# A Mamba block with a mixture of experts: softplus, router and buffers rearranged, and GpSimd's product by C as one operation for each state step

## What is computed

```python
xp, res = split(x @ W_in.T)                      # 512 and 512 channels
xc = silu(causal_conv4(xp) + conv_b)
B, C, dt = split(xc @ W_x.T)                     # 16, 16 and 1 per token
dt = softplus(dt @ W_dt.T + b_dt)                # 512 channels
h  = exp(-exp(A_log) * dt) * h + dt * B * xc     # scan over tokens; 512 channels x 16 states
y  = einsum(h, C) + D * xc                       # sum over the 16 states
x  = layernorm(x + silu(y + res) @ W_out.T)
p  = softmax(x @ router.T); w, idx = top_k(p, 2); w = w / (w.sum() + 1e-9)
x  = layernorm(x + sum_k w_k * expert_idx_k(x))  # w1: 256 -> 1024, gelu, w2: 1024 -> 256
```

## Time and profile before

| | |
|---|---|
| median of 3 runs | 1729.33 us (1729.17 to 1731.65) |
| the profiled execution: its own time | 1732.87 us |
| its span, first to last instruction | 1731.3 us |
| mean granted TensorE clock | 0.882 of full speed |
| busy: PE, DVE, ACT, POOL | 1373.5, 1191.1, 1046.8, 958.5 us |
| first scan starts, last scan ends | 82.3 and 1087.1 us |
| first product of the experts | 1167.8 us |

### The profile page before, as it was taken

The page is one execution under the profiler, slowest core; times in us unless marked ns, Lnnn a source line. Parts: engine busy times, 40 slices in busy tenths (PEclk is TensorE's granted clock), DMA queues, the critical chain, the costliest instruction groups (busy, mean ns, idle before and its releaser), DMA issues. The chain is left out here.

```text
span 1731.3 us, 29370 instructions
## 1 busy us (share of the span) xinstructions
PE 1373.5 (79%) x8770; PEld 1144.4 (66%) x8771; DVE 1191.1 (69%) x2152; ACT 1046.8 (60%) x1474; POOL 958.5 (55%) x823
## 2 busy tenths in 40 slices
PE   4487796796896797797888789618999999999950
PEld 1256575575675676675666677517888889898850
DVE  2377777777878778778768689335666666666648
ACT  1788888788868778868688777203333333333414
POOL 0088877787976877875777888441222222222228
PEclk8688898998988898888888889758999999999975
DMA  2032232232332232332232333166644441411125
GB/s 69 25 105 91 93 117 89 76 117 89 111 107 83 94 123 68 114 116 77 101 110 70 109 122 107 49 211 189 195 151 149 154 147 40 149 41 38 38 92 218
DMA packets 104873, 183.63 MB, mean 106 GB/s; under 512 B 13200, under 2 KB 40464, under 8 KB 104784
## 3 DMA queue, kind: packets, MB, share of 16 engines
q1 hardware_dynamic: 89968, 150.48, 26.7%
q0 software_dynamic: 9888, 27.29, 4.7%
q10 hardware_dynamic: 4928, 4.73, 0.8%
HBM read 121.23 MB, written 61.23 MB: 105 GB/s over the span
## 5 line engine op out<-in xcount | busy, mean ns | idle before, releaser
L1023 POOL TENSOR_TENSOR arena<-arena 128x1024 f32<-128x1024 f32 x256 | 610.4, 2389 | 105.7 <-DVE arena L798 94.9
L401 PE MATMUL d_ps<-ident,arena 128*128 128x128 f32 x2048 | 348.3, 298 | 84.7 <-DVE arena L798 74.8
L628 ACT ACTIVATE arena<-u_tok,b_tok 128x512 f32<-128x512 f32 x512 | 327.4, 712 | 140.0 <-PE d_ps L401 139.9
L401 PEld LDWEIGHTS d_ps<-ident,arena 128*128 128x128 f32 x2048 | 262.2, 153 | 222.4 <-issue 100.9
L798 DVE TENSOR_TENSOR_SCAN arena<-arena,d_ps 128x512 f32<-128x512 f32 x256 | 303.8, 1211 | 117.1 <-PE d_ps L401 115.4
L798 DVE TENSOR_TENSOR_SCAN arena<-arena,carry,d_ps 128x512 f32<-128x512 f32 x256 | 319.7, 1271 | 93.4 <-PE d_ps L401 91.0
L415 PE MATMUL y_ps<-ident,arena 128*128 128x128 f32 x2048 | 323.6, 288 | 12.7 <-POOL arena L1023 12.7
L1240 POOL DMA_INDIRECT expert_out<-y,dest x71 | 70.9, 999 | 378.3 <-PE xt_ps L1299 331.0
L638 ACT ACTIVATE arena<-dt,neg_a 128x2048 f32<-128x2048 f32 x128 | 255.3, 1995 | 24.7 <-DVE arena L798 24.5
L415 PEld LDWEIGHTS y_ps<-ident,arena 128*128 128x128 f32 x2048 | 258.8, 150 | 15.3 <-POOL arena L1023 15.2
L1273 ACT ACTIVATE h_t<-ht_ps 128x512 f32<-128x512 f32 x142 | 84.4, 595 | 303.7 <-PE ht_ps L1331 303.7
(11 more groups left out here) (165 smaller groups left out, 1639.6 us busy)
## 6 DMA issues: line engine op xcount, KB each, us to landing
arena<-c_rows SPq DMA_DIRECT2D x128, 256.0 KB, 3.1
weight_parts<-arena SPq DMA_DIRECT2D x128, 256.0 KB, 2.0
arena<-weight_parts SPq DMA_DIRECT2D x32, 1024.0 KB, 5.4
arena<-in_pieces SPq DMA_DIRECT2D x128, 128.0 KB, 2.4
xg<-expert_rows POOLq DMA_DIRECT2D x71, 130.0 KB, 2.4
c_y<-expert_out SPq DMA_DIRECT2D x16, 512.0 KB, 8.0
x_t<-in_x_t SPq DMA_DIRECT2D x8, 512.0 KB, 4.2
x_t<-in_x_tok SPq DMA_DIRECT2D x8, 512.0 KB, 4.6
```

Of the source, the lines that this page charges most:

```text
L401: last = nc.tensor.matmul(d_ps[:, c % 2, j * P:(j + 1) * P], ub[:, g % U_RING, j, c * P:(c + 1) * P], t.ident[:], start=True, stop=True, i ...
L628: nc.scalar.activation(ub[:, g % U_RING, j, :], u_tok[:, j, :], ACT.Identity, scale=b_tok[:, b % 2, j, n:n + 1]).then_inc(scaled, 1)
L1023: nc.gpsimd.tensor_tensor(h[:, g % H_RING, lo:hi, :], h[:, g % H_RING, lo:hi, :], c_row[:, g % C_RING:g % C_RING + 1, :].broadcast_to([P, ...
```

## The change

1. `times_c` is one operation of 2048 columns for each step, with one `carry` copy. It waits for the fourth scan, and `hc_done` counts once for each step; all four groups of `sum_states` wait for it. `SUM_AT` becomes 6 + k + max(0, 10 - k // 3) (the same from k = 30 on), and the ring of `h` has 5 tiles, not 4.
2. Softplus works in `pre`, not in `tmp`, and runs earlier: `z_parts` at n = 5 and 6, `soft_tail` at n = 7. `silu` and `y_silu` move to n = 2, ahead of `scale(g + 2)` in ACT's program; `y_silu` writes a tile of its own, `y_u`. The additions that make dt and dt times xc are four operations of 1024 columns, one behind each scan of n = 10. The taps lie one behind each scan at (11, 2) to (12, 3) and (0, 0) to (1, 1). `ut_out` is spread over n = 13 and 14.
3. The router picks from the logits themselves. DVE does max, index and one-hot (8 operations of 8 columns) at (3, 0); subtraction, denominator, weights and the product of the one-hot with the ranks go to POOL. All 8 indirect transfers of a block stand at n = 12 to 15. The last two operations of `variance` go to POOL. The halo's sums are made ahead, at n = 4 of the iteration before.
4. Buffers: `x_t` has 2 tiles, not 3. The raw weight pieces are loaded into the second half of `parts`, so a piece's load follows the store of the one two before it, one step ahead. `BANK_OF` has other banks, and block 0 uses four banks of `y_ps`, which is idle then.
5. `setup` no longer waits for its 12 loads: three groups with a semaphore each are waited for where they are used, and two of the loads are issued by ACT.

Core of the diff (the rest renames semaphores or moves lines as said):

```diff
-H_RING = 4
+H_RING = 5
...
-        SUM_AT = [6 + k + max(0, 6 - k // 3) for k in range(4 * STATE)]
+        SUM_AT = [6 + k + max(0, 10 - k // 3) for k in range(4 * STATE)]
...
                 def sum_states(b, k):
-                    pe.wait_ge(hc_done, 2 * g + half + 1)
+                    pe.wait_ge(hc_done, g + 1)
...
-            def times_c(g, half):
-                pool.wait_ge(scan_done, 4 * g + 2 * half + 2)
-                lo, hi = 2 * half, 2 * half + 2
+            def times_c(g):
+                pool.wait_ge(scan_done, 4 * g + 4)
                 if b % 2 == 0:
-                    nc.gpsimd.tensor_copy(carry[:, n, lo:hi].unsqueeze(2), h[:, g % H_RING, lo:hi, T - 1:T])\
+                    nc.gpsimd.tensor_copy(carry[:, n, :].unsqueeze(2), h[:, g % H_RING, :, T - 1:T])\
...
-                nc.gpsimd.tensor_tensor(h[:, g % H_RING, lo:hi, :], h[:, g % H_RING, lo:hi, :],
-                                        c_row[:, g % C_RING:g % C_RING + 1, :].broadcast_to([P, 2, T]), ALU.mult)\
+                nc.gpsimd.tensor_tensor(h[:, g % H_RING], h[:, g % H_RING],
+                                        c_row[:, g % C_RING:g % C_RING + 1, :].broadcast_to([P, EC, T]), ALU.mult)\
                     .then_inc(hc_done, 1)
...
-                def step_sizes():
-                    dve.wait_ge(ln_done, 2 * f + 2)
-                    nc.vector.tensor_tensor(dt[:, f % 2], dt[:, f % 2], tmp[:], ALU.add).then_inc(dt_done, 1)
-                    nc.vector.tensor_tensor(tmp[:], dt[:, f % 2], xc[:, f % 2], ALU.mult).then_inc(u_done, 1)
+                def add_sizes(half):
...
+                    nc.vector.tensor_tensor(dt[:, f % 2, lo:hi], dt[:, f % 2, lo:hi], pre[:, lo:hi], ALU.add)\
+                        .then_inc(dt_done, 1)
+                def inputs(half):
...
+                    last = nc.vector.tensor_tensor(y_u[:, lo:hi], dt[:, f % 2, lo:hi], xc[:, f % 2, lo:hi], ALU.mult)
...
+                def router_pick():
+                    for j in range(TT):
+                        last = nc.vector.max(top[:, j, :], logit[:, j, :])
+                    for j in range(TT):
+                        last = nc.vector.max_index(idx[:, j, :], top[:, j, :], logit[:, j, :])
+                    for j in range(TT):
+                        for k in range(TOPK):
+                            last = nc.vector.tensor_scalar(onehot[:, j, k, :], t.iota_ef[:], ek[:, j, k:k + 1], None,
+                                                           ALU.is_equal)
...
                 for n in range(STATE):
                     g = STATE * i + n
+                    if back and n == 2:
+                        y_silu()
+                    if front:
+                        if n == 2:
+                            silu()
+                        if n == 7:
+                            soft_tail()
                     if 0 <= g + LEAD < STEPS:
                         scale(g + LEAD)
                         decays(g + LEAD)
                     if scans:
                         high_part(g)
...
                     if 0 <= g - 1 < STEPS:
-                        times_c(g - 1, 1)
+                        times_c(g - 1)
                     if scans:
-                        times_c(g, 0)
                         low_part(g)
...
-                    if place and n >= 14:
-                        send_rows(i - 2, n - 14)
+                        if n >= 12:
+                            send_rows(p, n - 12)
```

More of the change, by code:

```diff
@@ L129, with bank_of @@
             **{u: 2 for u in ("in0", "in1", "in2", "in3")}}
+EARLY_BANK = {**{f"in{c}": 2 + c for c in range(4)}, **{f"ut{j}": 2 + j for j in range(4)}}
+BANKS = 6
+def bank_of(use, b):
+    return EARLY_BANK[use] if b == 0 and use in EARLY_BANK else BANK_OF[use]
 def bank_counts():
-    fills, count = [0, 0], {}
+    fills, count = [0] * BANKS, {}
     for i in range(-2, BLOCKS + 2):
-        for u, bank in BANK_OF.items():
+        for u in BANK_OF:
             b = i + BLOCK_OF[u]
             if 0 <= b < BLOCKS:
-                fills[bank] += 1
-                count[u, b] = fills[bank]
+                fills[bank_of(u, b)] += 1
+                count[u, b] = fills[bank_of(u, b)]
     return count
@@ L684, in yt_out @@
                     wait_filled(act, use, r)
[L685 removed]
+                    nc.scalar.copy(tmp[:, c, :], bank(use, r)).then_inc(m_freed[bank_of(use, r)], 1)
                 def btok_out():
@@ L944, in step @@
[L944 to L952 removed]
+                        if back:
+                            if at == (8, 2):
+                                residual(0)
+                            if at == (9, 3):
+                                residual(1)
+                            if at == (10, 0):
+                                variance()
@@ new lines, in step @@
+                        if front:
+                            if n == 0 and q < 3:
+                                tap(f, 2, q + 1)
+                            if at in ((0, 3), (1, 0), (1, 1)):
+                                tap(f, 3, 4 * n + q - 2)
+                            if f == 0 and at == (5, 0):
+                                diagonals()
+                            if at in ((10, 0), (10, 1)):
+                                add_sizes(q)
+                            if at in ((10, 2), (10, 3)):
+                                inputs(q - 2)
```

583 lines of the change are left out of this document (302 added, 281 removed).

## The result

The changed kernel takes **1771.66 us** (median of 4 runs, 1770.76 to 1777.71), the kernel before 1730.26 in the same session: a ratio of 1.0246, 95% interval 1.0222 to 1.0271. It is slower by 41 us; the forecast said 8 us faster and its range ended at 1762.

The account below looks back on a forecast made before the run. No engine bounds the kernel; what counts is who waits for whom. Terms +3.1 - 18 - 8 + 15 = -7.9 us gave 1725.0 from the profiled 1732.87, or 1722 against the median, range 1692 to 1762.

Parts of the forecast that it names:

- The beginning: Before the first scan: shorter load waits, separate banks and later taps bring the first scan to 64 us from 82.3, -18.
- The product: On POOL, one operation of 2048 columns takes 4.57 us, where two halves took 4.78.
- The end: Behind the last scan: product ends 5 us earlier, `turn_y` gives 3 back, transfers lose their 4.09 us wait; -8 together.
- The blocks: All eight blocks, reckoned step by step without the clock's term: 1008.1 us for 1005.0, so +3.1.
- the clock: PE's waits for the product in late steps lower its clock, low about 23% of the time: +15 us.
- the round: Steps 9 to 15 and next step 0: loop from fourth scan through product, group and `drive` to fourth scan, 7.3 us.
- the pick of the router: Rival: DVE's 8 router operations wait for product 2, 3.3 us in each of five blocks; 1738 us, chance 0.10.
- The half clock: Rival: product waits drop PE's clock in about three of four late steps, costing 44 to 50; 1752 us, chance 0.30.
- below 0.8 means 1752: Sign: a granted PE clock below 0.8 between 90 and 1070 us would show the slower clock case, 1752 us.
- Product 7: Full block: product behind softplus and `low_part(7)` ends 58.8 us from step 1's first scan; step 9 begins at 59.8.
- the clock stays up: Rival: PE's clock does not fall behind product waits, so the clock's term is 0; 1707 us, chance 0.14.
- the round never closes: Rival: PE reaches group (n, 0) only after the product has long ended, so late steps are shorter; 1699 us, chance 0.06.

Follow-up runs that it names:

- e6: Changed kernel with `low_part` not waiting for ACT's `high_part`, leaving out the low halves of the experts' weights: 1733.6 us, ratio 1.0035 to the kernel before.
- e1: Changed kernel with the product by C back in two operations of 1024 columns: 1670.4 us, ratio 0.9660 to the kernel before.
- e3: Changed kernel with late sums, the last term of `SUM_AT` staying at 4, not falling to 0: 1665.1 us, ratio 0.9631 to the kernel before.

## Why the prediction was wrong

Its sum, in the frame of the profiled execution, was 1725.0; that execution took 1770.99. The 46 us between them, step by step:

*The beginning* (-18): the first scan starts at 59.8 and not 64, so -22.5. The mechanism held, and here the forecast was too low in its gain; PE's first product starts at 7.76 for the 8.3 reckoned, and DVE waits 5.48 us ahead of the first scan where 15.52 stood.

*The product* of 4.57 us: measured 4.56.

```profile
L963 POOL TENSOR_TENSOR arena<-arena 128x2048 f32<-128x2048 f32 x128 | 584.0, 4563 | 93.2 <-DVE arena L751 87.2
```

*The end* (-8): -3.4. The last product ends 5.2 us behind the last scan, as the forecast said, but the last block's transfers begin at 1183.34, 55.0 behind it, where they began 58.6 behind it. The landings for which they waited no longer stand there. What takes up the rest wasn't tested; the single bank of `turn_y` (1.8 us from one to the next, the clock at 0.50 from 1142 to 1150 us) is one candidate.

*The blocks* (+3.1, with +15 for the clock: +18): **+63.6** against before. This is the step that failed. The block sums were 1008.1; measured 1068.5, with 137 for 128 in the full blocks and 134.4 for 123.9 in block 0. Against the forecast's step by step (mean of blocks 2 to 5, us, the forecast without its term for the clock, which is 1.9 a block):

| steps | 1 to 8 | 9 | 10 | 11 | 12 | 13 | 14 | 15 | 0 | sum |
|---|---|---|---|---|---|---|---|---|---|---|
| forecast | 59.8 | 8.4 | 11.9 | 8.4 | 7.7 | 7.0 | 8.1 | 8.9 | 7.9 | 128.1 |
| measured | 64.6 | 8.8 | 11.3 | 10.1 | 7.9 | 6.8 | 10.0 | 9.6 | 7.9 | 136.9 |

So the round itself was sized well: steps 12, 13 and 0 came within 0.3 us. Of the 8.8 us that were missed, 4.8 lie in steps 1 to 8 (the late end of step 8 and, in block 3, the pick of the router) and 4.3 in steps 11, 14 and 15. Four parts of it:

- *The clock* was sized at 15 by the mean of the earlier trace rows. Behind the waits for the product it costs up to 31. The half clock stood in the prediction, both as a term and as the first rival, but its price was taken from a share of the whole time. No run shows that term, nor a rule by which a wait of PE brings the clock down: that was the author's estimate. What the traces show are single places: a clock of 0.99, then of 0.50; here 1.00, then 0.56 and 0.50 behind the wait of 4.09 us, and 1.00 again from 809 to 812 us; and 27 of the 59 places at full clock, two of them behind waits of over 3 us. Here slow work stands where a scan waits for it: not 23% of the 59 places but 32 of them were slow in whole or part, and 67 us became 100. The tell I named was useless for the same reason: "below 0.8 means 1752" looks at a mean, which rose (0.882 to 0.893).
- *Product 7* was foreseen well: end at 58.8 us from the first scan of step 1, measured 59.6 in block 5 (802.20 less 742.64). But step 9 was to begin 1.0 us later and began 3.8 later. The quarter of PE's list behind group (7, 0) also holds four matmuls of the output projection (0.87 at full clock), which the sum left out, and all of it ran at half clock.
- *Products late behind ACT*, beyond number 7, had no term, although the `low_part` that stands ahead of a product can wait for ACT in any step (2.16 us in step 14 of block 5). e6 sizes all of POOL's wait for ACT, product 7's with it, at 38 us, of which some 12 are half clock counted above (by the same count e6 has 19 of it). Block 0 is no case apart: its step 8 took 17.7 us, with `low_part(7)` waiting 8.37 and DVE's scan 11.26, but the steps before it were short, and steps 1 to 8 took 60.1 us together, near the 59.8 of a full block's forecast; step 0 took 10.9 us and steps 9 to 15 took 63.4, where that forecast has 7.9 and 60.4.
- *The pick of the router* (a rival with 0.10, 17 us) did happen, in two of the blocks. Eight comparisons of 8 columns each:

```profile
482.76 6.68 DVE L832 TENSOR_SCALAR onehot<-iota_ef,ek 128x8 f32<-128x8 f32 x8 [0.16 <-DVE ek L827]
...
1026.29 6.53 DVE L832 TENSOR_SCALAR onehot<-iota_ef,ek 128x8 f32<-128x8 f32 x8 [0.16 <-DVE ek L827]
```

  The steps 3 of blocks 3 and 7 took 15.1 and 13.3 us, where those of blocks 2, 4, 5 and 6 took 7.7 to 8.2: some 13 us in sum, in which the lateness of a `low_part` has its part too (5.36 us of idle time at 483.25).

These parts overlap and are partly bounds, so they do not add up to the 46: the clock's 16 above its term, the 26 of e6 that are not clock and the pick's 13 make 55. How the 46 divide among them stays open. Two small slips of the sum changed nothing: the terms of the round add up to 7.24 us, not 7.3, and those of step 10 to 12.0, not 11.9.

The rivals: the half clock (1752) was right in kind and came nearest, 20 us short, since it took no account of late products. That the clock stays up (1707) is ruled out by the 32 slow places, and that the round never closes (1699) by PE's 166.9 us of waiting. The chance of slower, 0.38, leaned mainly on the clock. What the sum lacked most was a comparison with the change's own other half. The forecast set +3 for the blocks as the net of everything; in truth the rearrangement was worth -58 over the whole kernel (e1) and the whole product +101, and a forecast that works out each alone would have met the second number earlier: steps 12 to 15 at 4.5 to 7 us, which e3 shows, were out of reach in a round of 7.3.

## What to carry to other kernels

An operation that is made larger starts with its last input, not its first; before merging two halves, write down the loop that the merged one closes with whatever consumes it, and move the consumer back in its engine's list by the operation's length, and by the lateness that the operation inherits from others. Here one number in the list of sums was worth 107 us, and with it the merge cost nothing. Price a wait of TensorE with the slow work behind it too, and look for it at the places on the path: a mean clock doesn't show it (here it rose, from 0.882 to 0.893, with up to 31 us lost to the half clock). And when a consumer is moved by a rule in a list, work out where each late item stands after the edit: a first step of the rule may leave the one that matters in its place.

## What the runs showed of the hardware

DVE and POOL lengthen each other's operations in more cases than the addition with two inputs of the earlier trace rows. With POOL's product under way, the cast of 8 columns from SBUF to SBUF took 2.81 to 3.39 us in its six meetings where the shortest took 0.171, the longest comparison of 8 columns 4.57 for a median of 0.225, and additions of two SBUF inputs 2.97 to 4.67 for 1.19.

```profile
L858 DVE CAST pos<-rk x8: 171/3060/3390, 415.5 to 1182.3; 128x8 uint32<-128x8 f32 x8
L832 DVE TENSOR_SCALAR onehot<-iota_ef,ek x64: 217/225/4571, 345.5 to 1178.3; 128x8 f32<-128x8 f32 x64
L856 DVE TENSOR_REDUCE rk<-onehot x8: 184/186/219, 415.3 to 1182.1; 128x8 f32<-128x64 f32 x8
```

(Columns: the group, its count, then ns in the order shortest, median, longest.) The reduction, which six times began beside a product, kept its duration (0.185 to 0.192 us), and so did scans and taps with an input in PSUM (1.28 and 0.75 us at most). The longest comparison, 4.57 us, is as long as a product, 4.56 on the mean. The reverse is there too: product 10 of block 5 began while DVE was in a multiplication of two SBUF inputs (825.04 to 826.23) and took 5.41 us where the mean is 4.56.

```profile
825.20 5.41 POOL L963 TENSOR_TENSOR arena<-arena 128x2048 f32<-128x2048 f32 x1 [5.14 <-DVE arena L751]
```
